# Norms and weights of the next stage inside the feed-forwards, and the delta rule's chunk products on 48-row stacks

## The reference

```python
k = rotary(x @ Wk.T);  v = x @ Wv.T          # per head, 16 wide
def step(W, kv):                             # a chunk of 16 tokens
    kc, vc = kv
    z = kc @ W
    grad = kc.T @ ((z - vc) * 2 / (16 * 16))
    return W - grad, z
out = layernorm(all z) * gamma + beta
return out @ Wo.T
```

```python
gate, up = split(x @ ternary(w_gate_up).T)   # 256 -> 2 x 1024
h = silu(gate) * up
return rms_norm(h) @ ternary(w_proj).T       # 1024 -> 256
```

## Time and the profile before

| | |
|---|---|
| time, median of 3 runs | 4026.34 us (4024.76 to 4029.02) |
| the profiled execution, its own time | 4044.84 us |
| span of its trace | 4043.0 us |
| mean granted TensorE clock, as a share of 2.4 GHz | 0.955 |
| busy: TensorE, VectorE, ScalarE, GpSimd | 90%, 62%, 49%, 19% |
| ff2, from the span's start | 1074.2 to 1202.4 |
| ln3 | 1202.4 to 1221.6 |
| dr3: up to the first products | 1221.6 to 1288.8 |
| dr3: first products | 1288.8 to 1302.2 |
| dr3: loop, tiles 0 to 6 | 1302.2 to 1512.1 |
| ff4 | 1584.4 to 1711.8 |
| ln5 | 1711.8 to 1731.4 |

### The profile page before, as it was taken

How to read it: one execution, slowest core, us unless ns; L and a number is a source line. 1 busy time by engine, 2 the same in 40 slices (tenths; PEclk the granted TensorE clock), 3 DMA queues, 4 the chain that set the end, 5 groups by cost and what they waited for, 6 DMA issues and landing times. The chain is left out here.

```text
span 4043.0 us, 55040 instructions
## 1 busy us (share of the span) xinstructions
PE 3636.1 (90%) x19935; PEld 2559.5 (63%) x20020; DVE 2522.9 (62%) x4918; ACT 1987.3 (49%) x4137; POOL 762.7 (19%) x832
## 2 busy tenths in 40 slices
PE   6999999999387997867999999969799999999989
PEld 5878788787275986731333333248677777777767
DVE  5656566565653664537888888634576666666643
ACT  3555555554342332414777777722355555555532
POOL 1000000000131441310000000030144434444410
PEclk9999999999698997977999999989899999999999
DMA  1000000000000000011000000020000000000000
GB/s 51 11 7 11 11 5 11 11 5 2 32 1 20 1 0 3 1 44 44 20 16 17 17 16 17 1 80 1 22 8 11 11 5 11 11 7 9 2 32 22
DMA packets 32929, 61.42 MB, mean 15 GB/s; under 512 B 7186, under 2 KB 21522, under 8 KB 30842
## 3 DMA queue, kind: packets, MB, share of 16 engines
q1 hardware_dynamic: 32682, 58.12, 4.6%
HBM read 48.53 MB, written 9.18 MB: 14 GB/s over the span
## 5 line engine op out<-in xcount | busy, mean ns | idle before, releaser
L1495 DVE TENSOR_REDUCE ga5m_nm<-ga5m_M 128x1 f32<-128x1024 f32 x512 | 605.9, 1221 | 126.5 <-PE ga5m_M L1398 124.6
L1483 ACT ACTIVATE ga5m_pr<-ga5m_E 128x512 f32<-128x512 f32 x1024 | 558.5, 599 | 231.7 <-PE ga5m_E L1434 214.9
L376 PE MATMUL at_A<-at_pT,at_V 128*128 128x512 f32 (+3 forms) x1536 | 519.2, 488 | 7.4 <-issue 5.1
L319 POOL TENSOR_TENSOR at_prob<-at_prob,at_slope_row 128x128 f32<-128x128 f32 (+7 forms) x256 | 370.1, 1449 | 577.0 <-DVE at_prob L570 576.4
L376 PEld LDWEIGHTS at_A<-at_pT,at_V 128*128 128x128 f32 x1536 | 283.9, 190 | 248.7 <-issue 204.4
L464 ACT ACTIVATE at_pT<-at_T 128x512 f32<-128x512 f32 (+3 forms) x768 | 347.5, 488 | 107.2 <-PE at_T L417 105.9
L1398 PE MATMUL ga5m_M<-ga5m_K,ga5m_Q 128*128 128x512 bf16 x978 | 303.4, 389 | 61.4 <-DMA ga5m_Q<-in_zrows 38.9
L417 PE MATMUL at_T<-all_ident,at_prob 128*128 128x128 f32 x2304 | 336.4, 273 | 9.1 <-ACT at_pT L464 9.0
L1434 PE MATMUL ga5m_E<-ga5m_Q,ga5m_K 128*128 128x512 bf16 x986 | 336.1, 382 | 4.1 <-ACT ga5m_pr L1483 2.6
L1434 PEld LDWEIGHTS ga5m_E<-ga5m_Q,ga5m_K 128*128 128x128 bf16 x1024 | 98.9, 97 | 302.8 <-ACT ga5m_pr L1483 221.5
L417 PEld LDWEIGHTS at_T<-all_ident,at_prob 128*128 128x128 f32 x2304 | 268.1, 140 | 31.7 <-issue 8.9
(11 more groups left out here) (289 smaller groups left out, 8523.9 us busy)
## 6 DMA issues: line engine op xcount, KB each, us to landing
ga5m_Q<-ga_qs SPq DMA_DIRECT2D x96, 96.0 KB
at_raw_qk<-in_pqk SPq DMA_DIRECT2D x32, 256.0 KB, 2.8
at_raw_v<-in_pv SPq DMA_DIRECT2D x16, 256.0 KB, 3.1
at_raw_o<-in_po SPq DMA_DIRECT2D x32, 128.0 KB, 2.0
ga_qs<-ga5s_part SPq DMA_DIRECT2D x6, 512.0 KB
ga5m_K<-ga_ks SPq DMA_DIRECT2D x48, 48.0 KB
all_X<-in_x SPq DMA_DIRECT2D x1, 2048.0 KB
tq_raw<-in_gu SPq DMA_DIRECT2D x1, 2048.0 KB, 8.0
```

The lines of the kernel that those rows point to most:

```text
L319: nc.gpsimd.tensor_tensor(dst[:, 0:end], dst[:, 0:end], slope_row[n // 2 % 2][:, 0:end], ALU.add).then_inc(ramp_done, 1)
L376: mm = nc.tensor.matmul(bank[:, lo:GQ * P], V[b][:, kt, col:col + DH], pT[g][:, kt, lo:GQ * P], start=(kt == 0), stop=(kt == GQ * (g + 1) ...
L1483: nc.scalar.activation(pr[e % NR][:, :], Eb[e % 3][:, :], ACT.Exp, scale=scale).then_inc(e_done, 1)
L1495: nc.vector.tensor_reduce(nm[half % 2][:, m:m + 1], Mb[v % 2][:, :], AX.X, ALU.max, negate=True).then_inc(m_free[v % 2], 1)
```

## The change

- `normed_swiglu` takes `nxt`, the XT of the stage that follows. For each group whose new X is ready, it computes that norm inside the feed-forward: VectorE's statistics in steps 4 and 5 and normalising in 6 and 7 of the next group, GpSimd's power at step 5, the transposes (`turn_next`) after step 0 of the group after that, ScalarE's copies after step 1, the low part on VectorE if there is one. The transposes use the two banks of the group's own `turn` and of the square sums, so each of these waits for the others' readers. The last two groups come at the end. ff2 and ff4 have `nxt=[XT]`, ff6 the two parts. ln3, ln5 and ln7 are gone. `inverse` moves from step 0 to step 1.
- ff2 and ff4 issue at their start the loads of the next stage's rotary table and weights (`fetch`), into tiles held in a scope around them; `rotary_features` and `project_tokens` take these tiles.
- `delta_rule` has one block "p" for rotary, V projection and K transposes. ScalarE writes each tile's K and V rounded to fp32r (high part), VectorE the rest (low part), and SP stores both in DRAM, 256 KB each, 32 stores. GpSimd zeroes the stacks KS and KVS. After the last store come twelve loads of stacks for tile 0.
- A stack has 128 rows, 48 of them used: 16 rows for each of three part products (K high, low, high by KV high, high, low), for all 8 chunks of a tile. `product` is a fp32r matmul of a chunk of KS by one of KVS. `mask_k`, the chunk masks and KV are gone. In the loop SP reloads the stacks of a sequence for the tile that follows as soon as its last product is done; there is one buffer for each sequence. The loading of hm stands behind the twelve loads on SP's queue.

```diff
+            def turn_next(g):
+                pe.wait_ge(xl_done, min(g + 3, NG) * DC)
+                if rms:
+                    pe.wait_ge(ms_done, g + 1)
+                if g:
+                    pe.wait_ge(next_done, g * DC)
+                pe.wait_ge(nxn_done, (g + 1) * GT)
+                for c in range(DC):
+                    for j in range(GT):
+                        mm = nc.tensor.transpose(turned[c][:, j * P:(j + 1) * P], nxn[:, j, c * P:(c + 1) * P],
+                                                 consts["ident"][:, :])
+                    mm.then_inc(nturn_done, 1)
...
             def square_sums(g):
                 pe.wait_ge(acc_done, (g + 1) * (FC - 1))
+                if nxt is not None and g:
+                    pe.wait_ge(next_done, g * DC)
...
                 for f in range(FC):
                     gate_up(g, f)
+                    if nxt is not None and f == 0 and g >= 2:
+                        turn_next(g - 2)
...
+            if nxt is not None:
+                turn_next(NG - 2)
             down(NG - 1, 0)
             if rms:
                 square_sums(NG - 1)
             down(NG - 1, 1)
+            if nxt is not None:
+                turn_next(NG - 1)
...
+                if nxt is not None and g:
+                    if f in (4, 5):
+                        next_measure(g - 1, range(2 * f - 8, 2 * f - 6))
+                    if f == 5:
+                        next_shifted(g - 1)
+                    if f in (6, 7):
+                        next_normalise(g - 1, range(2 * f - 12, 2 * f - 10))
...
+        def load_stacks(sp, t, b):
+            rows = slice((b * QT + t) * P, (b * QT + t + 1) * P)
+            for i in range(3):
+                part = kvs[i == 1][rows, 0:D].rearrange("(j s) n -> s j n", s=C)
+                sp.dma_start(KS[b][C * i:C * i + C, :, :].bitcast(F32), part).then_inc(s_in[b], 16)
+                part = kvs[i == 2][rows, :].rearrange("(j s) n -> s j n", s=C)
+                sp.dma_start(KVS[b][C * i:C * i + C, :, :, :, :].rearrange("p j v c n -> p j (v c n)")
+                             .bitcast(F32), part
+                             ).then_inc(s_in[b], 16)
...
+                sp.wait_ge(zero_done, 2 * BATCH)
+                for i in range(NK):
+                    sp.wait_ge(stored[i], 16 * 2 * NT // NK)
+                for b in range(BATCH):
+                    load_stacks(sp, 0, b)
...
             @block.sync
             def _(sp):
-                sp.dma_start(masks[:, :], io["chunk"]).then_inc(m_in, 16)
                 sp.dma_start(hm[:, :, :], io["hm"]).then_inc(m_in, 16)
+                for t in range(1, QT):
+                    for b in range(BATCH):
+                        sp.wait_ge(pp_done, (t - 1) * NP + (b + 1) * DC * PC)
+                        load_stacks(sp, t, b)
...
                 def product(t, p):
-
                     q, pair = divmod(p, PC)
                     b, c = divmod(q, DC)
-                    pe.wait_ge(mk_done, t * (NCH * NC) + (q * NC + 2 * pair + 2))
+                    if c == 0 and pair == 0:
+                        pe.wait_ge(s_in[b], t * STACK + STACK)
                     if not (isinstance(t, int) and t == 0 and p < 2):
                         pe.wait_ge(ab_done, t * NP + (p - 1))
                     for e in range(2):
-                        mm = nc.tensor.matmul(PP[p % 2][:, e, :, :], MK[q % 2][:, 2 * pair + e, :],
-                                              KV[:, bass.ds(t + b * QT, 1), c, :, :].rearrange("p a v n -> p (a v n)"),
-                                              start=True, stop=True)
+                        mm = nc.tensor.matmul(PP[p % 2][:, e, :, :], KS[b][:, 2 * pair + e, c * P:(c + 1) * P],
+                                              KVS[b][:, 2 * pair + e, :, c, :], start=True, stop=True)
                     mm.then_inc(pp_done, 1)
```

More of the change, by code:

```diff
@@ L721, in normed_swiglu, with _ @@
         NF = NG * FC
+        if fetch:
+            @block.sync
+            def _(sp):
+                for tile, source, sem in fetch:
+                    sp.dma_start(tile, source).then_inc(sem, 16)
         @block.tensor
@@ L734, in turn @@
                         pe.wait_ge(ms_done, g - 1)
+                if nxt is not None and g >= 3:
+                    pe.wait_ge(next_done, (g - 2) * DC)
                 pe.wait_ge(xn_done, (g + 1) * GT)
@@ L828, in _ @@
                     high((F - 1) // FC, (F - 1) % FC)
+                if nxt is not None and f == 1 and g >= 2:
+                    copy_next(g - 2)
                 if f == 5 and g + 1 < NG:
@@ L831, in _ @@
             high(NG - 1, FC - 1)
+            if nxt is not None:
+                copy_next(NG - 2)
+                copy_next(NG - 1)
         @block.gpsimd
@@ L868, in _ @@
                     gather(F)
[L869 removed]
+                    if f == 1 and g:
                         inverse(g - 1)
+                if nxt is not None and f == 5 and g:
+                    next_root(g - 1)
             if rms:
                 inverse(NG - 1)
+            if nxt is not None:
+                next_root(NG - 1)
         @block.vector
@@ L946, in _ @@
                     low(F - 1)
+                if nxt is not None and len(nxt) == 2 and f == 1 and g >= 2:
+                    next_low(g - 2)
                 if f == 1 and g and rms:
@@ L963, in _ @@
             add(NG - 1, 0)
+            if nxt is not None:
+                next_measure(NG - 1, range(2))
             add(NG - 1, 1)
+            if nxt is not None:
+                next_measure(NG - 1, range(2, GT))
+                next_shifted(NG - 1)
+                next_normalise(NG - 1, range(GT))
+                if len(nxt) == 2:
+                    next_low(NG - 1)
 def hadamard_weights(nc, name, consts, io, w1, w2):
@@ L1551, in delta_rule @@
-        turn(nc, name + "k", kT, lambda c, g: KV[:, 4 * g:4 * g + 4, c, 0, :], consts, False)
+        KS = [o.sb(f"KS{b}", [P, NC, D], F32R) for b in range(BATCH)]
+        KVS = [o.sb(f"KVS{b}", [P, NC, 2, DC, P], F32R) for b in range(BATCH)]
+        s_in = [o.sem(f"s_in{b}") for b in range(BATCH)]
+        STACK = 16 * 6
+        def load_stacks(sp, t, b):
[7 more added lines that the diff above has]
+                             ).then_inc(s_in[b], 16)
@@ L1552, in delta_rule @@
         with Scope(nc, name + "m") as s:
-            masks = s.sb("masks", [P, NC])
             hm = s.sb("hm", [P, 2, P])
-            MK = [s.sb(f"MK{i}", [P, NC, P]) for i in range(2)]
             AB = [[s.sb(f"AB{i}{q}", [P, NC, 2, P]) for q in range(NCH)] for i in range(2)]
-            W = [[s.sb(f"W{q}{i}", [P, P]) for i in range(2)] for q in range(NCH)]
-            WB = [s.sb(f"WB{q}", [P, P]) for q in range(NCH)]
+            room = rotary[0][:, :, :].rearrange("p a n -> p (a n)")
@@ L1559, in delta_rule @@
+            W = [[room[:, (2 * q + i) * P:(2 * q + i + 1) * P] for i in range(2)] for q in range(NCH)]
+            WB = [room[:, (2 * NCH + q) * P:(2 * NCH + q + 1) * P] for q in range(NCH)]
             U = [s.ps(f"U{q}", [P, 4 * P]) for q in range(NCH)]
@@ L1778, in program @@
                 move_low(nc, kept, [w1l, w2l], moved, False)
-                normed_swiglu(nc, "ff6", X, consts, [w1h, w1l], [w2h, w2l], False, (moved, 32))
-            XT = parts(t, "XT", [P, DC, TOK])
-            layer_norm(nc, "ln7", X, XT, consts)
+                normed_swiglu(nc, "ff6", X, consts, [w1h, w1l], [w2h, w2l], False, (moved, 32), nxt=XT)
             causal_attention(nc, "at7", X, XT, consts, [io[x + "1"] for x in ("pqk", "pv", "po", "bqk")] + [None],
```

284 lines of the change are left out of this document (209 added, 75 removed).

## The result

The changed kernel takes 4085.61 us (median of 4, 4082.81 to 4086.91) against 4026.25; the ratio is 1.0145, interval 1.0131 to 1.0158. It is slower by 59 us. The forecast was 4051 us, slower by 25, with a range up to 4074: the side was right, and 34 of the 59 us were not in the forecast.

What follows compares the result with a forecast made beforehand. TensorE, busy nine tenths of the span, was taken to bound the kernel. Norms -1.4, weights -15, prelude -2.6, loop +42 and last tile +2 gave +25 on 4026.34: 4051 us, own range 4033 to 4074, whole range 3942 to 4074.

Steps and rivals of the forecast that it cites:

- the norms: ff2, ff4, ff6: moving norms inside removes 41.4 us and brings back 17, 17 and 6; net -1.4 us.
- the last tile: Delta rule's last tile, which began at full clock: costs 2 us more.
- the prelude: Delta rule before the loop: matrix work 48, stores 4, stack loads 15, products 11; 78 against 80.6, -2.6 us.
- the loop: Delta rule's seven tiles: pairs with short products stay at half clock, 4.28 us a step, 36.0 a tile; +42 us.
- the weights: Early loads for ga5's rotary, output projections of ga5 and dr3, and V projection: 15 us gained.
- a norm inside a ternary feed-forward: ff2 and ff4: transposes, VectorE work, waits and lower clock add 17 us each, between 8 and 24.
- The stack loads: Prelude: twelve loads, 2304 KB, after the last store; 15 us, bounded by 9 and 24.
- the long idle time ahead: Before the first products: TensorE, idle some 19 us during stores and stack loads, arrives cold.
- The 0.1 a step: Loop: changing type between pair and product can cost some 0.1 us a step, within the range 36 to 52.
- The baseline of a tile: Loop before the change: 209.9 us over seven tiles, 30.0 each.
- Full clock in the loop: First rival: VectorE sets 2.4 us a step, 21 a tile; -63 us, total 3944 us; chance 0.20.
- loads would set the pace: Second rival: full clock but stack loads give 24 to 25 us a tile; 3970 us; chance 0.10, partly full clock included.

Runs made afterwards that it cites:

- e10: Kernel before with MK and KV rounded to fp32r (short products, no low parts, no stacks): 4083.23 us, ratio 1.0137.
- e1: Kernel before, unedited, executed and traced a second time: 4027.21 us.
- e11: Changed kernel with e9, e5 and e3 together, plus three useless matmuls at each tile's boundary and none in the steps: 3929.47 us, ratio 0.9759.
- e3: As e2, plus useless matmuls ahead of and among the first 16 products, none in the loop: 4076.70 us.
- e9: As e2, with the 48 rows of each stack dealt out so each load writes sixteen rows eight apart: 4067.09 us.
- e4: As e3, plus one useless matmul in each step of the loop: 3989.89 us, ratio 0.9897.
- e7: As e4, with the third part of each stack in rows 64 to 79 instead of 32 to 47: 3990.89 us.
- e8: e7 and e5 together, plus one useless matmul a step in the last tile: 3973.77 us.
- e12: As e11, plus one useless matmul in each step: 3958.76 us, ratio 0.9827.
- e6: As e3, with the third part of each stack in rows 64 to 79: three executions at 4077.3 to 4077.5 us, one at 3959.73.
- e2: Changed kernel with the load of hm issued at the start of block p, ahead of stores and stacks: 4080.03 us, ratio 1.0132.
- e5: Changed kernel with ln3 and ln5 as passes of their own again, ff6 keeping its norm: 4059.26 us, ratio 1.0072.

## Why the forecast was too low, step by step

By the table 34.7 us were missing (59.7 - 25): 14.7 in the norms, 11.1 in the last tile, 6.5 in the prelude and 3.6 in the loop, less 1.2 in the weights and the start. Two steps failed: the last tile was priced at +2 from a stretch that only the traced execution had at half clock, and it was +13.1; and 17 us were put on a norm inside a ternary feed-forward, where the runs show 22 to 25. The stack loads, 15 us, were mis-sized as well; with hm they took 22.7.

**The loop at half clock: right.** Step 4.26 against 4.28, tile 35.8 against 36.0, and e10 shows that the short products by themselves do it. But the reason given beside it (the long idle time ahead) is not needed, since e10 waits 4.69 us ahead of its first products where the changed kernel waits 17.91. The other half, that the mixture stays at 0.50 because it is near the last tile, was drawn from one execution, and from a tile that in fact began at 1.00; e1 and e11 show that pairs alone, and the mixture, also run at 1.00. So the number came out right with a reason that was half luck. What the traces show is a state that the loop comes in with. From 0.50 it did not rise (the changed kernel, e3, e9, e10) unless useless matmuls stood beside the products in its steps (e4, e7, e8; in e8's last tile, which has them but no products, it stayed down). From 1.00 it stayed (e1, e11, e12) or was lost: behind the first step in e3 and e6, and in the last tile of the first trace of before, of e4 and of e8. All the losses came behind idle time at a boundary, but e1 had the same 0.83 us ahead of its last tile and kept the clock. What decides between the two stays open. The 0.1 a step that the range allows for a change of type rests on no run; 4.26 leaves no room for it.

**The baseline of a tile: off by 0.7.** I took the loop to begin at 1302.2 and divided 209.9 by seven. The first Z of that trace is five us later, at 1307.10; e1 has 205.06 us for seven tiles, 29.3 each. So the loop grew by 45.6 us, not 42. The same five us were missing in the prelude's 80.6.

**The last tile: +13.1, not +2. This step failed in its reasoning.** "All terms are differences, so I carry +25 to the median." The trace was of an execution 18.5 above the median, and I priced the last tile, which I cite as being at 0.50, from it. In e1 that tile runs at 1.00. The excess of 18.5 was known, and a term hung on it: the odd stretch at half clock should have been looked for, and the tile priced at 1.00 as well. This is 11 us of the 34.7 that were missing.

**The prelude: +3.9, not -2.6 (the table's +9.9, less the 6.0 us of rotary load wait that the forecast counts here and the table a row higher).** Matrix work 48 us as forecast (1229.82 to 1277.86), though some 3 us of it are the half clock at its start. The stores took 5.7 rather than 4, and the sixteen pairs of products 13.2 rather than 11 (1306.18 to 1319.38). Stacks and hm together took 22.7 rather than 15; I had the order of the queue right, and 24 as the upper bound, but leaned to the wrong side. e2 gives hm's place 5 us, e9 the rows 13.

**The norms: +12.3 and +10.8 for ff2 and ff4, not +4.2 each (from the table, with the 6.0 and 6.3 us of load wait taken out); ff6 -9.8 as forecast.** e5 gives 26 for the two together. With the second trace as the baseline the price inside a ternary feed-forward is 25 and 24 us (12.3 and 10.8 more than the 12.8 taken away), where I had 17 and a bound of 24. This is the largest part of what was missing, 14.7 us with ff6. But here too one execution is the baseline. Over all traces ff2 with its norm, up to the first rotary matmul, took 155.3 us in the mean with the norm inside (seven traces) and 145.9 with the norm apart and the weights fetched as well (four); for ff4 it is 155.6 and 145.8. That is 9.3 and 9.8 us, a price of 22 to 23, inside the bound of 24, and about 11 us missing instead of 14.7. What was under-counted is the waiting of TensorE in front of ready work: 11.9 us for nxn in ff2 and 5.5 at the square sums behind it, against 3.8 for these before. Which of the placements costs how much is read from the waits and was not taken apart by a run.

**The weights: right, -15.7 against -15.** Of the last row of the table, -17.7, ff6 is 9.8, the other 7.9 are the later loads of ga5; its rotary load is 6.3 and the stretch with dr3's Wo 1.5. None of the three was tested by a run of its own.

**Rivals.** Full clock in the loop did not come by itself, but e11 shows that it was within reach and worth it; its step was priced at 2.4 and is 2.26. That loads would set the pace was wrong: in the loop e4 never waited more than 0.5 us for a stack.

## What to carry to other kernels

Before taking work off the engine that is full, ask what its clock lives on: here a tile took 35.8 us with short products that came in at half clock, 29.3 with long ones at full clock, and 19.5 with short ones that came in at full clock, by useless matmuls at the start, and found no idle time at the boundaries. Moving work into another stage can cost clock behind it: the rotary features began at 0.51 with the norm moved and at 1.00 without. When a profiled execution is off its kernel's median by as much as the effect looked for, find the stretch that makes it so before pricing anything from it. When a load writes few neighbouring partitions, deal its rows out if the sum over rows allows it (9 us in the traces of e9), and put small loads that someone waits for ahead of the large ones (5 us in e2).

## What the hardware showed that was not expected

The same matmuls ran at either clock for long stretches: pairs of Z and U at 1.00 for 15.2 us in one execution and at 0.50 for 21 us in another of the same kernel, which had begun the tile at 1.00; e6 took 4077 us three times and 3959.73 once. Adding 56 useless matmuls to a full engine (e4) saved 87 us. Sixteen partitions standing eight apart took loads at about 210 GB/s, sixteen neighbours at 111. With TensorE busy for 241.80 of 250.6 us the clock did not come up from 0.50 in the changed kernel; with one more matmul a step (e4) it came back.
